# Low parts of four experts' weights by TensorE products in the routing stage, instead of subtractions on VectorE and GpSimd

## The reference

```python
x = x + (lowpass(gelu(x @ W1.T + b1)) @ W2.T + b2)
t = t + attention(layernorm(t))              # t: 4096 x 192
n = layernorm(t)
probs = softmax(n @ gate_w.T)                # 8 experts
p, idx = top_k(probs, 2); p = p / (sum(p) + 1e-8)
h = silu(n @ gate_bank[e]) * (n @ up_bank[e])     # 192 -> 384
t = t + sum_k p[k] * (h @ down_bank[idx[k]])      # 384 -> 192
```

## Time and profile before

| | us |
|---|---|
| three runs, median | 404.89 |
| the profiled execution, its time | 404.22 |
| its span, first to last instruction | 402.2 |
| front phase, start to the barrier | 0 to 123.8 |
| routing phase | 123.8 to 154.2 |
| expert phase, first instruction to last | 155.0 to 402.2 |
| TensorE busy | 358.2 (89% of the span) |
| VectorE busy | 264.1 (66%) |
| GpSimd busy | 261.6 (65%) |
| ScalarE busy | 216.5 (54%) |

### The profile page before, as it was taken

How to read it: one execution, slowest core, us unless ns; L and a number is a source line. 1 busy time by engine, 2 the same in 40 slices (tenths; PEclk the granted TensorE clock), 3 DMA queues, 4 the chain that set the end, 5 groups by cost and what they waited for, 6 DMA issues and landing times.

```text
span 402.2 us, 8666 instructions
## 1 busy us (share of the span) xinstructions
PE 358.2 (89%) x2302; PEld 342.7 (85%) x2303; DVE 264.1 (66%) x726; ACT 216.5 (54%) x508; POOL 261.6 (65%) x270
## 2 busy tenths in 40 slices
PE   5987778799986996799999999999999999999990
PEld 4887667688886885699999999999999999999980
DVE  2577758999797997265666666666656666566650
ACT  3475844888561372245555555555555555555540
POOL 3047547788732005457878888887888788888763
PEclk9998898999999865799999999999999999999996
DMA  5999750235554100224544444454444444444432
GB/s 171 260 319 364 264 217 1 93 114 162 157 171 117 9 0 1 69 50 72 75 76 71 81 72 71 70 75 74 74 79 70 70 74 76 70 81 73 72 39 29
DMA packets 39419, 41.07 MB, mean 102 GB/s; under 512 B 13789, under 2 KB 32448, under 8 KB 39392
## 3 DMA queue, kind: packets, MB, share of 16 engines
q0 software_dynamic: 13824, 16.98, 26.0%
q1 hardware_dynamic: 25568, 23.78, 19.2%
HBM read 25.76 MB, written 14.98 MB: 101 GB/s over the span
## 4 chain that ended last, share of the span: by engine, by line
PE 56%; DMA 3%; issue 1%; POOLq 0%; POOL 0%; ACT 0%; DVE 0%; SPq 0%; ACTq 0%; DVEq 0%
PE moe_ps_y L1170 10%; PE moe_ps_h L1156 6%; PE moe_ps_gt L1145 3%; PE moe_ps_gt L1147 3%; PE moe_ps_gt L1149 3%; PE moe_ps_gt L1148 3%; PE moe_ps_gt L1146 3%; PE moe_ps_u L1145 3%; PE moe_ps_u L1148 3%; PE moe_ps_u L1146 3%; PE moe_ps_y L1172 3%; PE moe_ps_u L1149 3%; PE moe_ps_u L1147 3%; PE moe_ps_x L1136 2%; PE moe_ps_x L1137 2%; PE moe_ps_y L1169 2%
## 5 line engine op out<-in xcount | busy, mean ns | idle before, releaser
L1109 POOL DMA_INDIRECT out<-moe_y,idx_map x71 | 112.9, 1591 | 29.0 <-issue 20.1
L1101 POOL DMA_INDIRECT moe_xt<-rows,idx_map x71 | 74.3, 1046 | 54.8 <-POOLq L926 28.3
L1254 ACT ACTIVATE moe_yy<-moe_ps_y,moe_xt 128x384 f32<-128x384 f32 x71 | 41.4, 583 | 70.3 <-PE moe_ps_y L1170 70.3
L1170 PE MATMUL moe_ps_y<-wd,moe_h_hi 128*128 x213 | 70.0, 353 | 0.6 <-DVE moe_h_lo L1326 0.5
L1334 DVE TENSOR_TENSOR moe_y<-moe_yy 128x192 f32<-128x192 f32 x71 | 25.5, 360 | 55.8 <-ACT moe_yy L1254 55.8
L1234 ACT ACTIVATE moe_x_hi<-moe_ps_x 128x256 fp32r<-128x256 f32 x71 | 27.3, 385 | 38.8 <-PE moe_ps_x L1137 38.8
L1310 DVE TENSOR_TENSOR moe_x_lo<-moe_ps_x,moe_x_hi 128x128 fp32r<-128x128 f32 x71 | 20.7, 292 | 32.1 <-ACT moe_x_hi L1234 32.1
L1326 DVE TENSOR_TENSOR moe_h_lo<-moe_ps_h,moe_h_hi 128x384 fp32r<-128x384 f32 x71 | 39.6, 558 | 2.7 <-ACT moe_h_hi L1246 0.6
L1170 PEld LDWEIGHTS moe_ps_y<-wd,moe_h_hi 128*128 128x128 f32 x213 | 40.2, 189 | 1.2 <-issue 1.2
L1320 DVE TENSOR_TENSOR moe_hid<-moe_ps_u,moe_sg 128x384 f32<-128x384 f32 x71 | 38.9, 548 | 0.0
L1172 PE MATMUL moe_ps_y<-wd,moe_h_lo 128*128 x142 | 35.5, 250 | 0.0
(11 more groups left out here) (230 smaller groups left out, 968.1 us busy)
## 6 DMA issues: line engine op xcount, KB each, us to landing
w_lo<-in_wgu SPq DMA_DIRECT2D x8, 768.0 KB, 15.7
xs<-in_x SPq DMA_DIRECT2D x8, 388.0 KB, 8.6
rows<-front_xr SPq DMA_DIRECT2D x8, 384.0 KB, 2.7
out<-xs SPq DMA_DIRECT2D x8, 384.0 KB, 3.5
wd<-in_down SPq DMA_DIRECT2D x8, 288.0 KB, 4.3
xta<-in_xT SPq DMA_DIRECT2D x8, 256.0 KB, 5.5
moe_xt<-rows,idx_map POOLq DMA_INDIRECT x71, 2.8
out<-moe_y,idx_map POOLq DMA_INDIRECT x71, 3.6
```

The source lines that it names most:

```text
L1101: nc.gpsimd.indirect_dma_start(xt[:, slot, :], None, rows.ap(), bass.IndirectOffsetOnAxis(ap=idx_map[:, j, 0:1], axis=0)).then_inc(gathere ...
L1109: nc.gpsimd.indirect_dma_start(out, bass.IndirectOffsetOnAxis(ap=idx_map[:, j, 1:2], axis=0), y[:, j % YR, :], None, compute_op=ALU.add).t ...
L1170: ins = nc.tensor.matmul(both, hi, halves, start=(k == 0), stop=(k == 2))
L1254: nc.scalar.activation(yy[:, s].rearrange("p h c -> p (h c)"), ps_y[:, s, 0:2 * C], ACT.Copy, scale=xt[:, slot, bass.ds(GC + e, 1)]).then_ ...
```

## The change

- `READY` goes from 5 to 4. The subtractions of expert 4 leave the front phase, the three at the front phase's end and the six at the expert phase's start go.
- In the routing phase TensorE makes the twelve low parts of experts 4 to 7: for each 512-column piece an ordinary product of the unit matrix with the original plus a product of the negated unit matrix with the high part, in one PSUM accumulator (two accumulators of 1024 columns). The negated product is F32R for the 768-column parts and ordinary for the 576-column ones. ScalarE copies each result over the original. Four parts stand before the counting products in TensorE's order, eight behind them, and all stand before the one-hot products; on ScalarE all twelve copies stand before the one-hot loop.
- The filling products of the routing phase (10 and 30) go; each one-hot step but the first gets two products of 64 columns.
- The counting products wait for the triangular matrix alone (`tri_in`), no longer for all six tables.
- For the last two quads, `vtmp` and `minus` of `deviation` are made on VectorE (`late_parts`) instead of GpSimd.
- The expert phase begins with 24 filling products instead of 11, and its first products wait for `change_done` instead of `ready`.

```diff
+APART = 2
+AHEAD_OF_COUNTS = 4
-READY = 5
+READY = 4
...
# front phase, GpSimd, deviation(q)
+                    if q < QUADS - APART:
                         ... vtmp, minus as before ...
+                    else:
+                        pool.wait_ge(parts_done, q - (QUADS - APART) + 1)
...
# front phase, VectorE
+                def late_parts(q):
+                    s = q % RING
+                    dve.wait_ge(mv_done, made(q))
+                    dve.wait_ge(dev_done, freed(q))
+                    nc.vector.tensor_scalar(vtmp[:, s, :], mv[:, s, :, 1], EPS, None, ALU.add)
+                    nc.vector.tensor_scalar(minus[:, s, :], mv[:, s, :, 0], -1.0, None, ALU.mult).then_inc(parts_done, 1)
...
                     if n:
                         residual(n - 1)
+                    if n > QUADS - APART:
+                        late_parts(n - 1)
                     weights(n)
...
                 residual(last)
+                late_parts(last)
...
-                for e in range(READY, EXPERTS):
-                    split(e)
...
# routing phase
+        parts = []
+        for e in range(READY, EXPERTS):
+            parts += [(w_lo[:, e, 0], wa_hi[:, e]), (w_lo[:, e, 1], wb_hi[:, e]), (wd[:, e, 1], wd[:, e, 0])]
...
# ScalarE
+                def low_part(n):
+                    low = parts[n][0]
+                    act.wait_ge(low_made, n + 1)
+                    nc.scalar.activation(low, ps_low[:, n % RING, 0:low.shape[1]], ACT.Copy).then_inc(low_out, 1)
+                nc.scalar.activation(neg[:], eye[:], ACT.Copy, scale=-1.0).then_inc(negated, 1)
+                act.wait_ge(filled, 1)
+                nc.scalar.activation(oner[:], ones[:], ACT.Copy)
                 act.wait_ge(diff_done, 1)
                 nc.scalar.activation(pr[:, EARLY:T], lg[:, EARLY:T], ACT.Exp)
+                low_part(0)
                 act.wait_ge(second_done, 1)
                 nc.scalar.activation(red[:, 5, EARLY:T], red[:, 4, EARLY:T], ACT.Exp).then_inc(ex_done, 1)
+                act.wait_ge(tri_in, 16)
+                nc.scalar.activation(trir[:], trit[:], ACT.Copy).then_inc(exact, 1)
+                for n in range(1, len(parts)):
+                    low_part(n)
                 act.wait_ge(consts_in, 16 * len(consts))
...
# TensorE
-                keep_busy(10)
+                def low_product(n):
+                    low, high = parts[n]
+                    width = low.shape[1]
+                    if n >= RING:
+                        pe.wait_ge(low_out, n + 1 - RING)
+                    for at in (slice(0, 512), slice(512, width)):
+                        into = ps_low[:, n % RING, at]
+                        nc.tensor.matmul(into, eye[:], low[:, at].bitcast(F32), start=True, stop=False)
+                        minus = (neg[:], high[:, at]) if n % 3 < 2 else (neg[:].bitcast(F32), high[:, at].bitcast(F32))
+                        ins = nc.tensor.matmul(into, *minus, start=False, stop=True)
+                    ins.then_inc(low_made, 1)
+                pe.wait_ge(negated, 1)
+                for n in range(AHEAD_OF_COUNTS):
+                    low_product(n)
                 ... the two counting products ...
-                keep_busy(30)
+                for n in range(AHEAD_OF_COUNTS, len(parts)):
+                    low_product(n)
                 for q in range(TILES // HT):
+                    if q:
+                        for _ in range(2):
+                            nc.tensor.matmul(ps_p[:, 0:64], order_of, order_of[:, 0:64], start=True, stop=True)
                     pe.wait_ge(hot_a_done, q + 1)
...
# expert phase
-                keep_busy(11)
+                keep_busy(24)
                 turn_x(0, 0)
                 keep_busy(4)
-                pe.wait_ge(ready, 1)
+                pe.wait_ge(change_done, 1)
...
-                for e in range(READY, EXPERTS):
-                    for low, high in ((w_lo[:, e, 0], wa_hi[:, e]), (wd[:, e, 1], wd[:, e, 0])):
-                        ins = nc.vector.tensor_tensor(low, low.bitcast(F32), high.bitcast(F32), ALU.subtract)
-                ins.then_inc(ready, 1)
```

More of the change, by code:

```diff
@@ L140, in program @@
                         x, xT, w1, w2, lowpass, wgu, down, ytab, ident, wqkv, gate, rope, iotas[1], out)
-            routing_phase(nc, lg, choice, tri, iotas, row_tiles, idx_map, e_j, out, scattered)
+            routing_phase(nc, lg, choice, tri, iotas, row_tiles, idx_map, e_j, out, scattered, eye, wa_hi, wb_hi, w_lo, wd)
         expert_phase(nc, eye, rows, out, wa_hi, wb_hi, w_lo, wd, idx_map, e_j, scattered)
@@ L224, in front_phase @@
         early_chain = a.sem("early_chain")
+        parts_done = a.sem("parts_done")
         early_less, early_second, early_ex, early_chosen, early_gates = (
@@ L673, in deviation @@
                     s, at = q % RING, bass.ts(q, QT)
[L674 to L678, removed]
+                    if q < QUADS - APART:
+                        pool.wait_ge(mv_done, made(q))
+                        pool.sem_inc(pool_turn, 1)
+                        nc.gpsimd.tensor_scalar(vtmp[:, s, :], mv[:, s, :, 1], EPS, None, ALU.add).then_inc(eps_done, 1)
+                        nc.gpsimd.tensor_scalar(minus[:, s, :], mv[:, s, :, 0], -1.0, None, ALU.mult).then_inc(mean_done, 1)
+                        pool.wait_ge(eps_done, made(q))
+                    else:
+                        pool.wait_ge(parts_done, q - (QUADS - APART) + 1)
                     pool.sem_inc(pool_turn, 1)
@@ L682, in deviation @@
                     pool.wait_ge(pow_done, made(q))
-                    pool.wait_ge(mean_done, made(q))
+                    if q < QUADS - APART:
+                        pool.wait_ge(mean_done, made(q))
                     pool.sem_inc(pool_turn, 1)
@@ L887, in choose_experts, with routing_phase @@
     tt2(gates[:, at], tmp[:], tmp2[:], ALU.add).then_inc(gates_done, 1)
-def routing_phase(nc, lg, choice, tri, iotas, row_tiles, idx_map, e_j, out, scattered):
+def routing_phase(nc, lg, choice, tri, iotas, row_tiles, idx_map, e_j, out, scattered, eye, wa_hi, wb_hi, w_lo, wd):
     E, T = EXPERTS, TILES
@@ L917, in routing_phase @@
         ps_p, ps_t, ps_m = (a.ps(n, [P, 512]) for n in ("ps_p", "ps_t", "ps_m"))
+        neg, ps_low = a.sb("neg", [P, P], F32R), a.ps("ps_low", [P, RING, 1024])
+        negated, low_made, low_out, tri_in = (a.sem(n) for n in ("negated", "low_made", "low_out", "tri_in"))
+        parts = []
+        for e in range(READY, EXPERTS):
+            parts += [(w_lo[:, e, 0], wa_hi[:, e]), (w_lo[:, e, 1], wb_hi[:, e]), (wd[:, e, 1], wd[:, e, 0])]
         consts_in, gates_out, filled = (a.sem(n) for n in ("consts_in", "gates_out", "filled"))
@@ L923, in routing_phase @@
         hot_done, hot_a_done, map_done = a.sem("hot_done"), a.sem("hot_a_done"), a.sem("map_done")
-        consts = [(trit, tri)] + list(zip((io, first, idp, no_row, no_place), iotas[:1] + iotas[2:]))
+        consts = list(zip((io, first, idp, no_row, no_place), iotas[:1] + iotas[2:]))
         with nc.Block() as block:
@@ L928, in _ @@
             def _(sp):
+                sp.dma_start(trit[:], tri).then_inc(tri_in, 16)
                 for dst, src in consts:
@@ L1087, in expert_phase @@
         x_hi_done, x_lo_done, x_lob_done = a.sem("x_hi_done"), a.sem("x_lo_done"), a.sem("x_lob_done")
-        ready, change_done = a.sem("ready"), a.sem("change_done")
+        change_done = a.sem("change_done")
         silu_done, hid_done, weighed = a.sem("silu_done"), a.sem("hid_done"), a.sem("weighed")
@@ L1257, in _ @@
                 nc.scalar.activation(sg[:, 0, 0:1], eye[:, 0:1], ACT.Silu)
-                act.wait_ge(ready, 1)
+                act.wait_ge(change_done, 1)
                 x_high(0, 0)
```

4 lines of the change are left out of this document (1 added, 3 removed).

## The result

The changed kernel is slower: 423.49 us, median of six runs, against 403.6 for the kernel before, ratio 1.0401 with a 95% interval of 1.035 to 1.0451. Three of the six took 427 to 430 us, and the one of them that has a trace ran at the low clock already in the front phase; the ratio leaves those out (1.0401 x 403.6 = 419.8), and the rows of after come from a later execution of the same kernel without that, of span 417.1. The forecast was 408, with a range of 404 to 411.5: the sign of the likeliest case holds, the size does not.

The account below looks back on a forecast made before the run. VectorE was taken to pace the front phase and routing, TensorE the 71 tiles. 404.2 - 1.4 (front phase) + 9.4 (routing) - 4.6 (expert phase's start) = 407.6, 408.3 on the median's level, given as 408; range 404 to 411.5.

Parts of the forecast that it names:

- the likeliest case: Whole kernel: the forecast itself, slower at 408 us, chance 0.45.
- The product sum: Routing phase: twelve parts take 22.2 us of TensorE, 1.73 or 2.1 each, counting products 0.6; last part ready at 147.0.
- Rival 3: Routing phase: unit-matrix products cost one pass like F32R, parts 7.7 us together, loop never waits; 396.8 us, chance 0.06.
- The loop held back: Routing phase: one-hot steps queue behind all parts, VectorE idles some 7 us after four steps; step 4 comes 9.8 later.
- Two products of 64 columns (about 0.12 each and 0.64 - tail for the step) just fit: One-hot loop: the added pair fits beside TensorE's step, so the loop keeps VectorE's pace of 0.97 us a step.
- rival 1: Expert phase's start: TensorE's clock low, fillers 6.1 us, 2 us of gain gone; 409.6; chance 0.25.
- The added 64-column products speak against a fall in the loop: One-hot loop: the added products were taken as evidence against TensorE's clock falling there; a fall would cost about 2 us.
- The gather: Expert phase's start: subtractions held the first gather at 5.63 us; without them it takes 0.98 and lands 4.65 sooner.
- Rival 2: Expert phase's start: 5.63 us is a first gather's price and stays, about 0.6 of 4.6 remains; 411.6; chance 0.12.
- The first tile's -1.3: Expert phase: first turn to second `gate_product` takes 4.3 us at the high clock instead of 5.6, -1.3.
- The front phase: Front phase's loop: fewer subtractions and a wait gone shorten it by 1.4 us, bounds 0.4 to 2.4.
- signs of being right: Trace: last copy about 146, VectorE idle some 7 us, gather about 1 us, PEclk 1.0, turn bound by 24 fillers.

Follow-up runs that it names:

- e3: Changed kernel with two F32R products of 512 columns in place of the two of 64 columns ahead of each one-hot step; ratio 1.0156 to the kernel before.
- e2: Changed kernel without the two 64-column products ahead of each one-hot step; ratio 1.0182 to the kernel before.
- e7: Kernel before with only the two 64-column products added ahead of each one-hot step but the first; ratio 1.0124, +5.0 us.
- e9: Changed kernel with nine parts, expert 4's three low parts and their products left out; ratio 1.0366 to the kernel before.
- e4: Kernel before with six low parts made by products, no loop products, 11 fillers, old front phase; ratio 0.9875, median 396.04 us.
- e8: Changed kernel with 11 filling products instead of 24 at the expert phase's start; ratio 1.0325 to the kernel before.
- e12: Changed kernel without the one-hot loop's two products and with 11 filling products instead of 24; ratio 1.0085 to the kernel before.
- e6: Kernel before without the six subtractions at the expert phase's start and their wait, six low parts left out; ratio 0.9841, -6.4 us.
- e5: Kernel before with the change's front phase edit alone, expert 4's low parts left out; ratio 0.9963, -1.5 us.
- e1: The changed kernel again, no edit; ratio 1.0433 to the kernel before.
- e10: Repeat of e4: kernel before with six low parts made by products, no loop products, 11 fillers; ratio 0.9903, median 397.96 us.
- e11: Kernel before with six parts by products, the front phase's late_parts and wide loop products; one run 394.92 us, five 404.9 to 410.37, no ratio.

## Why the prediction was wrong

**The product sum: right.** From 121.26 to 143.06 + 0.39 = 143.45 the twelve parts and the two counting products take 22.2; the forecast was 22.2 and 0.6. (Its addends make 22.3, and 124.2 + 7.3 makes 131.5 and not 131.3 for the counting products; neither bears on the result.) A 768-column part takes 1.63 to 1.74 (1.73 forecast), a 576-column one 2.11 (2.1). Rival 3, a unit-matrix product at the price of an F32R one, falls with it: at PEclk 1.00 an ordinary product of 512 columns takes 0.86 (136.60 - 135.74), 1.68 ns a column, an F32R one by an estimate 0.44 (a part's 1.63, less 768 x 1.68 ns, over 768). The rows shown of before give 1.87 to 1.93 ns a column with the tail; the lower price that the lower end of the forecast's own range (405.5) allows for stands in no run before the result, and after has the 1.68 in its place.

**The loop held back: right.** VectorE stands 7.20 behind its fourth step, "some 7 us" forecast; its scan comes 1.8 later after the phase's start (7.95 against 6.13; "about 2"), step 4 comes +9.11 (+9.8 forecast).

**"Two products of 64 columns (about 0.12 each and 0.64 - tail for the step) just fit": this is the step that failed**, with the term that rival 1 set on it. Two things were wrong. The pair was priced by columns, 0.24 in all; the rows of after read as a price by weight loads. The pair is two ordinary products, four instructions of 64 columns, and takes 0.45; the step is four F32R products of 72 columns, takes 0.45 too, and PEld is busy without a gap. So each instruction costs about the load of its 128x128 weights, 0.11 at the high clock (0.45 / 4) and 0.21 at the low one (0.85 / 4), where PEld's groups of four loads follow each other 0.86 apart (150.39 - 149.53); no run leaves the loads out, so this cause is read from the rows and not tested. And the fit was worked out at the high clock alone, where it does hold (0.90 of 0.97; e3, 0.91). At the low clock the four one-hot instructions alone take 0.86. Without the pair the loop still keeps its pace there (0.98 a step in before and in e2), but only 0.11 of its 0.97 is free, and the pair wants 0.85: a step grows to 1.71. The rows of before had the last ten steps at the low clock already (9.80 / 10, PEclk 0.50 in 143.3 to 152.6). The loop takes 18.23 instead of 11.74 and TensorE's backlog behind it costs a further 3.65: 10.1 together, where the forecast had nothing for the pair and -0.4 for the tail. e2 takes the pair away and gets 10 us back; e7 adds it alone and loses 5.

**"The added 64-column products speak against a fall in the loop": wrong.** The clock fell early in TensorE's loop in after (PEclk 0.76 in 146 to 148) and in e9 (0.70 in 140 to 142), later in e7 (0.62 in 138 to 140), and did not come back, in after with TensorE busy all of 10.00 us in 150 to 160. It fell about as early in e2 and e4, which have no such products (by the fifth step; PEclk 0.50 in 150 to 152 and in 138 to 140), so the fall does not need them either. What decides the fall isn't settled by these runs.

**Rival 1** named the right mechanism, a low clock around the joint, and mis-sized it: "a fall within the loop costs about as much" as 2 us. It costs 10.1 in the loop; the term it did work out, the 24 fillers at the low clock, came on top. They took 7.22 where the forecast had 4.2 and rival 1 had 6.1, since more of them ran at the low clock: by the prediction's own 0.35 and 0.175 some 17 of the 24 (an estimate from the 7.22), where rival 1 had 10.5. The 13 added ones cost 3.4 and 1.9 by the traces of e8 and e12 and about 4 by the ratios.

**The gather: right.** 1.06 against 5.63, and e6 shows that the subtractions made the difference; without them and their wait the kernel before is 1.6% faster. Rival 2 falls. In what way subtractions on VectorE hold a gather on GpSimd no run shows; the runs show its length with them (5.63) and without (1.06, and 1.05 in e6). But the freed time did not reach the end: with 24 fillers mostly at the low clock the turn comes only 0.43 sooner after `idx_map`, where the forecast had 3.3. The first tile's -1.3 came (-1.25, at PEclk 1.00).

**The front phase: right, with its end left out.** VectorE's last operation of the phase, the end of `gates`, comes at 116.52 against 120.26; 2.45 of that was there at the first `scores` already (52.18 against 54.63, start-up, which the change does not touch and which differs from execution to execution), so the loop gained 1.29 (1.4 forecast) and e5's 1.26. What stands behind it was left out: the phase ends with twelve filling products, and in the traces of after and e5 those ran at the low clock, +1.7, so that the phase itself ended only 0.4 sooner net of the start-up. Since e6 has the same +1.7 with the old front phase, that is no price of the edit; over its runs e5 gives -0.4%, 1.5 us.

**In sums.** The terms were -1.4, +9.4 and -4.6, together +3.4; the trace has -2.88, +19.25 and -1.68, with 0.21 in the rest +14.9. Of the 11.5 between the totals, 9.85 lie in routing (10.1 by the pair and 0.4 for the tail that was not gained, less 0.7 for a loop start a little sooner than forecast), 2.9 at the expert phase's start (the fillers), and the front phase takes 1.5 off, by an early start-up. Without the 2.45 of start-up the two traces differ by 17.3, and the runs of e1 by 17.4 (1.0433 of 402.77).

**The signs.** All that the prediction named as signs of being right came: 7.20 of idle time, a gather of 1.06, PEclk 1.00 in the parts (121.3 to 143.4) and in the first tile, the turn at the end of the 24 fillers, and the last copy at 143.48, which is 145.9 with the 2.45 of start-up put back ("about 146"). None of them looked at the loop's pace or at the fillers' clock, and there the forecast failed.

## What to carry to other kernels

Price a filler that is to fit under another engine's pace at both clock levels: where the rows show the stretch at the low clock even once, the lower level decides, and a step that takes 0.86 of a pace of 0.97 there has no room (with the pair it took 1.71). Do not price narrow products by their columns alone: in these rows instructions of 64 and of 72 columns cost the same, about a weight load each (0.11 at the high clock, 0.21 at the low one). And count cover in front of an in-order queue by when its first waiting step is due: six parts that end before that are a gain (e4, e10), twelve are a loss even with neither the pair nor the added fillers (e12, 1.0085). The six further parts had little to win: the front phase's edit that goes with them is worth 1.5 us (e5).

## What the runs showed of the hardware that was not expected

An engine that its record shows busy without a gap can stay at the low clock: 0.50 granted in 148 to 160 of after and, by the slices, up to about 177, with PE busy 10.00 of 10.00 us in 150 to 160, while with wide F32R products in their place (e3) it stayed at 1.00 through the same loop, and in e11 the same wide products lost it (0.50 in 136 to 158). All three came to the loop with the same idle time of 1.34 behind ScalarE's first one-hot step, so that alone does not decide. The twelve fillers at the front phase's end ran at 1.00 in some executions (2.60) and mostly at the low clock in others (4.26 and 4.28; PEclk 0.50 in 120 to 122 of e5), with the front phase's edit (e5) and without it (e6). Which of the two comes is a matter of several us in this kernel, and what sets it stays open.
